# Token lists of a mixture-of-experts router: bf16 one-hots, seven node tiles an operation, on four engines

## The reference, cut to what matters

```python
logits = xf @ router_w                       # 6250 x 8 experts
gate_vals, idx = jax.lax.top_k(logits, 2)
gates = jax.nn.softmax(gate_vals, axis=-1)
for e in range(8):
    h = jax.nn.relu(xf @ w1[e] + b1[e]) @ w2[e] + b2[e]
    y = _layernorm(xf + h, gamma[e], beta[e])
    w = jnp.sum(jnp.where(idx == e, gates, 0.0), axis=-1)
    out = out + w[:, None] * y
```

## Time and profile before

| | us |
|---|---|
| three timed runs | 3389.63, 3393.13, 3393.44 (median 3393.13) |
| the profiled execution | 3388.69 |
| its span in the profile | 3386.8 |
| routing block in it | about 2614 to 2718 |
| expert block in it | 2718.6 to the end |

### The profile page before, as it was taken

One profiled execution on the slowest core, in us unless ns is written; L12 is line 12 of the kernel. 1 busy time (PEld: TensorE's weight loads), 2 busy tenths in 40 slices (PEclk: granted clock), 3 DMA queues, 4 the chain that ended last, 5 costly groups with the idle time before them and its releaser, 6 DMA issues. The chain is left out here.

```text
span 3386.8 us, 72877 instructions
## 1 busy us (share of the span) xinstructions
PE 2831.9 (84%) x13006; PEld 1590.8 (47%) x13007; DVE 2141.7 (63%) x5667; ACT 1467.3 (43%) x3801; POOL 1742.0 (51%) x1834
## 2 busy tenths in 40 slices
PE   4979989999994788888888888999896777777774
PEld 4945556666663222223333333444443555555452
DVE  4557788777777445555566666666665746665665
ACT  2545521111110455555555555565554034444443
POOL 1245611222222577776776666666664046666664
PEclk9999999999997899999999999999998589999998
DMA  4335510011111577666776777767775335555554
GB/s 164 89 129 163 164 38 25 31 43 43 50 55 38 150 200 205 199 199 203 211 211 209 216 210 208 219 208 219 218 217 192 140 66 89 88 88 87 88 90 63
DMA packets 225186, 467.83 MB, mean 138 GB/s; under 512 B 65633, under 2 KB 78292, under 8 KB 223863
## 3 DMA queue, kind: packets, MB, share of 16 engines
q0 software_dynamic: 100592, 320.33, 35.7%
q1 hardware_dynamic: 124551, 147.04, 14.2%
HBM read 387.23 MB, written 79.90 MB: 138 GB/s over the span
## 5 line engine op out<-in xcount | busy, mean ns | idle before, releaser
L939 POOL DMA_INDIRECT rows<-h_rows,idx x954 | 948.6, 994 | 489.1 <-issue 250.7
L1052 PE MATMUL acc_ps<-rows,W 128*128 128x512 f32 x1908 | 985.1, 624 | 181.8 <-DMA rows<-h_rows,idx 165.0
L1052 PEld LDWEIGHTS acc_ps<-rows,W 128*128 128x128 f32 x1908 | 304.4, 189 | 802.4 <-issue 540.3
L977 ACT ACTIVATE e_pos<-pqb,es_col 128x128 f32<-128x128 f32 x954 | 372.8, 391 | 156.7 <-issue 89.8
L1155 DVE SCALAR_TENSOR_TENSOR W<-window,dst_col,e_top 128x128 f32<-128x128 f32 x954 | 297.5, 350 | 221.7 <-PE acc_ps L1052 219.4
L978 ACT ACTIVATE e_neg<-pqb,es_col 128x128 f32<-128x128 f32 x954 | 367.9, 386 | 0.0
L699 DVE TENSOR_SCALAR masked<-p_window,dst_col,hi_col 128x128 f32<-128x128 f32 x954 | 281.6, 365 | 43.6 <-DVE p_window L691 41.4
L1149 DVE TENSOR_TENSOR e_top<-e_pos,e_neg 128x384 f32<-128x384 f32 x318 | 172.4, 555 | 190.4 <-ACT e_neg L978 169.4
L972 ACT COPY idx<-src_col 128x2 int32 x477 | 87.3, 188 | 460.9 <-SPq L921 458.9
L676 POOL MEMSET top<- 128x768 f32 x48 | 35.4, 738 | 471.8 <-DVE folded L707 471.8
L1450 POOL DMA_INDIRECT xs<-xf_rows,idx_get x105 | 141.8, 1351 | 230.5 <-DVE z L1567 112.9
(11 more groups left out here) (251 smaller groups left out, 4667.3 us busy)
## 6 DMA issues: line engine op xcount, KB each, us to landing
lo_row<-src_lo SPq DMA_DIRECT2D x102, 256.0 KB, 3.2
rows<-h_rows,idx POOLq DMA_INDIRECT x954, 3.8
xb<-in_x SPq DMA_DIRECT2D x49, 256.0 KB, 2.6
h_rows<-hb SPq DMA_DIRECT2D x49, 256.0 KB, 2.1
fold_w<-in_x SPq DMA_DIRECT2D x49, 256.0 KB, 2.6
res_rows<-fold_w SPq DMA_DIRECT2D x49, 256.0 KB, 2.0
a_own<-h_rows SPq DMA_DIRECT2D x49, 256.0 KB
a_xr<-res_rows SPq DMA_DIRECT2D x49, 256.0 KB
```

Source lines behind the costliest of these rows:

```text
L939: nc.gpsimd.indirect_dma_start(G[j][:], None, h_rows, bass.IndirectOffsetOnAxis(ap=idx[:, j:j + 1], axis=0)).then_inc(row_in[j], 16)
L977: nc.scalar.activation(e_pos[:, half, j, :], pqb[s][:, 0, :], ACT.Exp, bias=es_col[:, ds(at_tile + (half * HT + j), 1)])
L1052: nc.tensor.matmul(acc_ps[s][:], W[:, j, :], G[j][:], start=(opens and j == 0), stop=(j == VT - 1), skip_group_check=True).then_inc(row_us ...
```

## The change

The sum over nodes is made in seven chunks of `QT` = 7 node tiles.

- `hi`, `lo` and a copy `iota16` of the column numbers are bf16. VectorE makes the one-hots of a chunk in four operations: `hot_hi` for each `k`, [128, 7, 105], and `hot_lo` for each `k`, [128, 7, 128], each by comparing `iota16`, repeated over the tiles, with `hi` or `lo`, each value repeated along the columns. Both are plain zeros and ones now.
- A node's number is split into its row in the tile (plus one) and the tile. GpSimd multiplies `hot_hi` by the row number (`named[..., 0, :]`), two operations a chunk; ScalarE multiplies it by the tile number (`named[..., 1, :]`), seven operations a chunk.
- TensorE does 14 matmuls a chunk, `hot_lo` against the 210 columns of `named`: 98 of bf16 in place of 196 instructions of f32 in the trace and two of zeros. Columns 0 to 104 of the sum hold the rows, 105 to 209 the tiles; one more VectorE operation puts them together.
- All buffers of the chunks are double. VectorE waits at chunk c for GpSimd, ScalarE and TensorE at chunk c - 2; GpSimd and ScalarE wait for `hot_hi` and for TensorE at chunk c - 2.
- The loops over tiles are gone: all chunks are written out. The steps for `expert_of` come after the chunks. The memset of `zero16` goes, and the constant `node_no` (49 columns) becomes `row_no` (one).

```diff
-        "node_no": np.arange(NT)[None, :] * P + np.arange(P)[:, None] + 1,
+        "row_no": np.arange(P)[:, None] + 1,
...
                     def _(pool):
-                        nc.gpsimd.memset(zero16[:], 0.0).then_inc(zero_ready, 1)
...
+                        for c in range(NT // QT):
+                            b = c % 2
+                            pool.wait_ge(hi_ready, c + 1)
+                            if c >= 2:
+                                pool.wait_ge(hot_used, c - 1)
+                            for k in (0, 1):
+                                last = nc.gpsimd.tensor_scalar(named[b][:, k, :, 0, :], hot_hi[b][:, k], C["row_no"], None, ALU.mult)
+                            last.then_inc(row_named, 1)
...
+                        for c in range(NT // QT):
+                            b = c % 2
+                            act.wait_ge(hi_ready, c + 1)
+                            if c >= 2:
+                                act.wait_ge(hot_used, c - 1)
+                            for j in range(QT):
+                                last = nc.scalar.activation(named[b][:, :, j, 1, :], hot_hi[b][:, :, j, :], ACT.Copy, scale=float(c * QT + j))
+                            last.then_inc(tile_named, 1)
...
-                        pe.wait_ge(zero_ready, 1)
-                        nc.tensor.matmul(token_ps[:, 0:P], zero16[:], zero16[:], start=True, stop=False, skip_group_check=True)
-                        with pe.Fori(0, NT) as t:
+                        for c in range(NT // QT):
+                            b = c % 2
+                            pe.wait_ge(lo_ready, c + 1)
+                            pe.wait_ge(row_named, c + 1)
+                            pe.wait_ge(tile_named, c + 1)
                             for k in (0, 1):
-                                pe.wait_ge(hot_ready, 2 * t + k + 1)
-                                nc.tensor.matmul(token_ps[:, 0:P], hot_lo[k][:], hot_hi[k][:], start=False, stop=False, skip_group_check=True).then_inc(hot_used, 1)
-                        nc.tensor.matmul(token_ps[:, 0:P], zero16[:], zero16[:], start=False, stop=True, skip_group_check=True).then_inc(tokens_done, 1)
+                                for j in range(QT):
+                                    last = nc.tensor.matmul(token_ps[:, 0:2 * ST], hot_lo[b][:, k, j, :], named[b][:, k, j].rearrange("p o s -> p (o s)"),
+                                                            start=(c + k + j == 0), stop=(c == NT // QT - 1 and k == 1 and j == QT - 1))
+                            last.then_inc(hot_used, 1)
...
+                        step(V.tensor_copy(iota16[:], C["iota_row"]))
...
+                        for c in range(NT // QT):
+                            b = c % 2
+                            if c >= 2:
+                                dve.wait_ge(row_named, c - 1)
+                                dve.wait_ge(tile_named, c - 1)
+                                dve.wait_ge(hot_used, c - 1)
+                            for hot, of, w, ready in ((hot_hi, hi, ST, hi_ready), (hot_lo, lo, P, lo_ready)):
+                                for k in (0, 1):
+                                    last = V.tensor_tensor(hot[b][:, k], iota16[:, 0:w].unsqueeze(1).broadcast_to([P, QT, w]),
+                                                           of[:, k, c * QT:(c + 1) * QT].unsqueeze(2).broadcast_to([P, QT, w]), ALU.is_equal)
+                                last.then_inc(ready, 1)
...
-                        with dve.Fori(0, NT) as t:
-                            for k in (0, 1):
-                                dve.wait_ge(hot_used, 2 * t + k + 1)
-                                V.tensor_scalar(hot_hi[k][:], C["iota_row"], hi[:, k, ds(t, 1)], None, ALU.is_equal)
-                                V.tensor_scalar(hot_lo[k][:], C["iota_row"], lo[:, k, ds(t, 1)], C["node_no"][:, ds(t, 1)],
-                                                ALU.is_equal, ALU.mult).then_inc(hot_ready, 1)
-                        dve.wait_ge(tokens_done, 1)
...
+                        dve.wait_ge(hot_used, NT // QT)
+                        step(V.tensor_scalar(unlisted[:, 0:ST], token_ps[:, 0:ST], 0.0, C["nobody"], ALU.is_equal, ALU.mult))
+                        step(V.scalar_tensor_tensor(token_f[:, 0:ST], token_ps[:, 0:ST], -1.0, unlisted[:, 0:ST], ALU.add, ALU.add))
+                        step(V.scalar_tensor_tensor(token_f[:, 0:ST], token_ps[:, ST:2 * ST], float(P), token_f[:, 0:ST], ALU.mult, ALU.add))
+                        step(V.tensor_copy(token_of[:, 0:ST], token_f[:, 0:ST]))
```

More of the change, by code:

```diff
@@ L1259, in gps_layer @@
                 slot_f, listed_i, part_i = sb(ro, "slot_f", [P, 2, NT]), sb(ro, "listed_i", [P, 2, NT], I32), sb(ro, "part_i", [P, 2, NT], I32)
-                hi, lo = sb(ro, "slot_hi", [P, 2, NT]), sb(ro, "slot_lo", [P, 2, NT])
+                hi, lo = sb(ro, "slot_hi", [P, 2, NT], BF16), sb(ro, "slot_lo", [P, 2, NT], BF16)
+                iota16 = sb(ro, "iota16", [P, P], BF16)
                 at_or_past, owner = sb(ro, "at_or_past", [1, ST, NE]), sb(ro, "owner", [1, ST])
-                hot_hi, hot_lo = ([sb(ro, f"{n}{k}", [P, P]) for k in (0, 1)] for n in ("hot_hi", "hot_lo"))
-                zero16 = sb(ro, "zero16", [P, P], BF16)
+                QT = 7
+                assert NT % QT == 0 and NT < P
+                hot_lo, hot_hi = ([sb(ro, f"{n}{b}", [P, 2, QT, w], BF16) for b in (0, 1)] for n, w in (("hot_lo", P), ("hot_hi", ST)))
+                named = [sb(ro, f"named{b}", [P, 2, QT, 2, ST], BF16) for b in (0, 1)]
                 gates = sb(ro, "gates", [P, 2, NT])
@@ L1269, in gps_layer @@
                 weight_ready, nobody_ready, kept = sem("r_weight_ready"), sem("r_nobody_ready"), sem("r_kept")
-                r_step, dif_ready, exp_ready, picks_ready, picks_counted, hot_ready, hot_used, zero_ready, tokens_done = (
-                    sem("r_" + n) for n in ("step", "dif_ready", "exp_ready", "picks_ready", "picks_counted", "hot_ready", "hot_used",
-                                            "zero_ready", "tokens_done"))
+                r_step, dif_ready, exp_ready, picks_ready, picks_counted, lo_ready, hi_ready, row_named, tile_named, hot_used = (
+                    sem("r_" + n) for n in ("step", "dif_ready", "exp_ready", "picks_ready", "picks_counted", "lo_ready", "hi_ready", "row_named",
+                                            "tile_named", "hot_used"))
                 with nc.Block() as block:
@@ L1314, in _ @@
                         steps = Steps(dve, r_step, 0)
-                        dve.sem_inc(hot_used, 2)
                         def step(ins):
@@ L1388, in _ @@
                         step(V.tensor_copy(expert_of[:], owner[:]))
-                        with dve.Fori(0, NT) as t:
-                            for k in (0, 1):
-                                dve.wait_ge(hot_used, 2 * t + k + 1)
-                                V.tensor_scalar(hot_hi[k][:], C["iota_row"], hi[:, k, ds(t, 1)], None, ALU.is_equal)
-                                V.tensor_scalar(hot_lo[k][:], C["iota_row"], lo[:, k, ds(t, 1)], C["node_no"][:, ds(t, 1)],
-                                                ALU.is_equal, ALU.mult).then_inc(hot_ready, 1)
-                        dve.wait_ge(tokens_done, 1)
-                        step(V.tensor_scalar(unlisted[:], token_ps[:, 0:P], 0.0, C["nobody"], ALU.is_equal, ALU.mult))
-                        step(V.scalar_tensor_tensor(token_f[:], token_ps[:, 0:P], -1.0, unlisted[:], ALU.add, ALU.add))
-                        step(V.tensor_copy(token_of[:], token_f[:]))
+                        dve.wait_ge(hot_used, NT // QT)
[3 more added lines that the diff above has]
+                        step(V.tensor_copy(token_of[:, 0:ST], token_f[:, 0:ST]))
             with ExitStack() as ep:
```

## The result

The changed kernel took 3356.97 us (median; 3354.48 to 3361.19), the kernel before beside it 3391.38: 34.4 us less, a ratio of 0.9895 (95% interval 0.9881 to 0.991). The forecast was 39.9 us less, with 3353.2 as the time. The sign and the range held; the stretch that the sum was made for is 7.3 us longer than it said. The range from 3340 to 3372 would have held for rivals B and D as well, so the time alone does not tell which of them is at work; the trace does.

A forecast was written before the change was run, and what follows sets the result against it. Routing loop bound by VectorE's and TensorE's waits for each other; new loop is VectorE's work plus GpSimd's holds, ending 2677.1: 2717.2 - 2677.1 - 0.2 = 39.9 us saved, 3353.2 against the 3393.13 median; range 3340 to 3372, 8 in 10.

The forecast's parts named there:

- B: Rival, loop: no engine hinders another, 4.33 us a chunk, 44.0 us saved, 3349 (3343 with GpSimd at 1.15); 30%.
- D: Rival, loop: weight loads not hidden, two chunks cost 12.3 us, 30 us saved, 3363; 11%.
- Ahead of the loop: Before the loop: `iota16` copy adds 0.2 us; the four `expert_of` steps, 2.9 us, move behind it at no cost.
- VectorE in the loop: Four comparisons a chunk, 0.92 and 1.08 us, at a pace of 0.84 and 1.00: 3.68 us a chunk, 25.8 for seven.
- GpSimd alone: Two multiplies of 735 elements a chunk, 2.04 us each, chosen over 1.15 for the bf16 type: 4.08 us a chunk.
- What VectorE and GpSimd do to each other: In the loop: GpSimd holds VectorE off 0.70 us an instruction, making 3.68 + 1.40 = 5.08 us a chunk, 35.6 for seven.
- After the loop: Behind the loop: one more VectorE step (0.3 us), fewer columns in the others (-0.1); expert stage unchanged at 668 us.
- A: The forecast's own sum, VectorE's work plus GpSimd's holds in the loop: 39.9 us saved, 3353; 40%.
- C: Rival, loop: GpSimd and VectorE alternate whole instructions, 7.76 us a chunk, 21.6 us saved, 3372; 9%.
- E: Rival, loop start: fetch of the straight-line code waits for the weight loads' end, chain starts 19 us late, 3372; 3%.
- F: Rival, loop: GpSimd pays for each run of 105 as an instruction, 14 multiplies 92.6 us, 18 slower, 3411; 3%.
- G: Rival, stretch's end: the weights' write, landing at 2657.6, becomes the end; 54 to 59 us saved, 3334 to 3339; 4%.

The follow-up runs named there:

- the experiment: Changed kernel with the four `expert_of` steps ahead of the chunks again: 31.5 us less than the kernel before (3352.90 against 3384.39; 0.991).
- the first experiment: Changed kernel with the column numbers copied to PSUM, one SBUF input per comparison: 3344.83 against 3384.39 us for the kernel before (0.9889); stretch 36.4 us.
- the f32 kernel: Changed kernel with f32 tiles in place of bf16, still seven node tiles an operation: 10.2 us less than the kernel before (0.9966), stretch 65.1 us.
- the kernel with the shortest stretch: Changed kernel with column numbers in PSUM and a second operation in GpSimd's multiply: 3332.64 against 3383.41 us for the kernel before (0.9851); stretch 28.6 us.

## Why the prediction was right in sign and size, and where it failed

- **Ahead of the loop.** The `expert_of` steps were right (-2.8 for -2.9); they are hidden as said, and worth 2.5 us by the experiment. The `iota16` copy was mis-sized: 0.57 us for 0.2, so the two together give -2.2 for -2.7. It ran beside GpSimd's memset and ended 0.08 us behind it; the copy of the same 128 numbers to PSUM, beside the same memset, took 0.30 in the first experiment.
- **VectorE in the loop.** Right: 0.92 and 1.08 us, and a pace of 3.68 (pairs of 1.76 and 2.09 us). The doubled rate for bf16 did not come, and the f32 kernel showed the same 0.92 and 1.08. The Trainium skill (Vector Engine (DVE) Microarchitecture Reference, 5.1 Performance modes) wants an innermost step of one in every source for it, and this operand repeats each value: the trace agrees, with 0.92 us in either type, though no run has this comparison without the repeat. The tier table of the Trainium skill (VectorE: DVE Perf Modes, The perf-mode tier table), taken by itself, has 1224 ns in bf16 for 2293 in f32; by that ratio I estimate 0.49 us.
- **GpSimd alone.** The term was right (2.13 us for 2.04), its reason wrong: not the type but the form of the instruction, shown by 2.13 in f32 and 0.97 with two operations. That the wrong reason gave the right size is luck.
- **ScalarE and TensorE.** Right: 1.99 us and 2.61 a chunk, for "2.0 to 2.5" and 2.6. Rival D, weight loads not hidden, would have made TensorE 4.7. ScalarE was busy 3.98 us of the 11.8 us turn, which is why it could take the row multiply.
- **What VectorE and GpSimd do to each other: the step that failed.** Of its two halves the first was right in size and wrong in number: a multiply that holds VectorE up does so for about 0.6 us, not for its 2.13 (the long comparisons are 1.518 for 0.92, and `at_or_past` 1.62 for 1.02). The sum had 0.70 of it for each of the 14 multiplies, 9.8 us; the trace has four comparisons held up, 2.4 us in all. The second half was seen and then left out of the sum. I had the row of 1.56 us for 0.81, wrote "it waited", and gave it no term. It costs GpSimd 1.72 us in the first multiply of a turn (3.852 for 2.133) and 1.11 in the second (3.242), so 2.8 us in each 11.8. With GpSimd at 11.33 of 11.8 us, GpSimd with its waits is the bound, and not "VectorE's work plus GpSimd's holds". Per chunk that is 5.9 for 5.08. VectorE's last comparison ended 39.2 us into the stretch for 35.6, mostly for waits for buffers, and GpSimd's last multiply outlasted it by 4.0 us for 0.3: 3.6 and 3.7 make the 7.3. The PSUM experiment takes the mutual waits away and lands at 36.4 us.
- **After the loop.** Right: 0.3 us, and the expert block is as long as it was (669.5 for 668.2; 666.3 to 668.0 in the experiments on chips of that speed). What the routing block saves is kept, as far as timings tell: in profiled executions the block (from `top_logit` to the step behind the chunks, 103.0 us before) got 12 to 50 us shorter, and the timed gain differed from that by up to 4.5 us either way, and by 6.4 for one tile an operation.
- **The rest of the difference.** Timed, the change brought 34.4 us, profiled 32.3. A profile is of one execution: that of the kernel before lay 2.7 us below its median (3388.69 for 3391.38), that of the changed kernel 0.7 (3356.28 for 3356.97). The stages ahead of the block and the expert block, which the change does not touch, moved by about one microsecond each, in opposite directions.

The rivals. B had a stretch of 34.6 us; it is neared (36.4) only when the hindrance is removed. The changed kernel, at 46.0, lies between A (38.7) and C. C, whole-instruction exclusion, had the stretch at 57 us (2638.4 to 2695.4); here a comparison is held 0.6 us of the multiply's 2.13, so it is refuted as it stands. D had 48.6, nearer to the 46.0 than A, but by TensorE's 4.7 us a chunk, which took 2.61. The Trainium skill (SBUF — State Buffer, SBUF: two separate sides) says that such a pair lock each other out for the whole instruction: the trace agrees that VectorE's two SBUF inputs count (moving one input to PSUM ended it for the comparisons), and that GpSimd waits, by 0.6 to 2.5 us. It disagrees on the comparisons, which are let in after 0.6 of the 2.13. E did not come: the chain reached its first one-hot at 2637.28, for 2638.4 forecast, and VectorE's chain did not stand still for some 19 us. F did not come either: a 735-element multiply in seven runs is 2.13, so a run costs nothing extra. The write of G had landed by 2655.8, 27 us ahead of the end of the stretch; in the kernel with the shortest stretch it landed near 2652.0 and the stretch ended at 2661.70, still 10 us behind it.

What stays open is what decides how many VectorE instructions GpSimd sits out: 0.6 to 1.7 us of waiting were seen with the one-operation multiply, 2.5 with the two-operation one. I didn't try other spacings of VectorE's instructions. What in the chip is at work can't be said either, only what ends it.

## What to carry to other kernels

When work goes to GpSimd beside a busy VectorE, count both directions: what GpSimd holds up, and how long it waits before each instruction, since the second sets the pace once GpSimd is near full. Look for a VectorE input that can sit in PSUM, or give the work to ScalarE, before adding buffers; a buffer more did nothing here until the hindrance was gone. And a cheap row in the trace for another form of the same operation is worth a try: here 0.97 us for 2.13.

## What the hardware showed that I had not expected

- GpSimd's multiply by a per-partition scalar costs 2.13 us for 735 elements as one operation, in bf16 and in f32 alike, and 0.97 us with a second multiply by one. The one-operation rows fit 0.28 us and 2.5 ns an element (0.546 for 105, 2.13 for 735, 2.84 for 1024; a row of the kernel before has 1.51 for 512, where the line gives 1.56).
- Two engines that hinder each other do so unequally: VectorE lost 0.6 us to a multiply, whether of 2.13 or 0.97 us, GpSimd 0.6 to 2.5 us to VectorE's comparisons and the like. A single PSUM operand on VectorE's side ended both. Small VectorE steps with one SBUF input could be held up as well, to the end of GpSimd's instruction (a copy of 128 beside a memset 0.57 us for 0.30 into PSUM; a cast of 105 beside a multiply 0.75 for 0.20).
- An f32 matmul of 210 columns, two records, ran at 0.35 us a record at the lower granted clock (0.50) and at 0.177 at the higher (1.00); a bf16 one, one record, at 0.187 at the lower. The f32 loop was granted 1.00 for part of its time, the bf16 loop of the changed kernel 0.50 all the time.
- The kernel before took 3383 to 3391 us on some chips and 3565 to 3599 on two others, and the changed kernel's stretch was 46.0 us on one of either kind.
